# Second cross attention: the row of negated maxima by a matmul with the identity

## What is computed

```python
qn = layernorm(x, ln_q_g, ln_q_b)
q = qn @ Wq * scale                    # 16 heads of 64
k, v = jnp.split(media @ Wkv, 2, axis=-1)
sim = jnp.einsum('bhid,bhjd->bhij', q, k)
sim = jnp.where(media_mask[:, None, None, :], sim, neg_inf)
attn = jax.nn.softmax(sim, axis=-1)
out = jnp.einsum('bhij,bhjd->bhid', attn, v)
```

## Time and profile before

| | |
|---|---|
| median of 3 runs | 3642.56 us |
| profiled execution, span | 3628.6 us |
| TensorE busy in the span | 3390.8 us (93%) |
| VectorE busy | 2019.1 us (56%) |
| ScalarE busy | 1846.1 us (51%) |
| GpSimd busy | 1589.9 us (44%) |
| diagonals of the stage (L1823) | 64, median 1349 ns |

### The profile page before, as it was taken

One profiled execution on the slowest core, in us unless ns is written; L12 is line 12 of the kernel. 1 busy time (PEld: TensorE's weight loads), 2 busy tenths in 40 slices (PEclk: granted clock), 3 DMA queues, 4 the chain that ended last, 5 costly groups with the idle time before them and its releaser, 6 DMA issues. The chain is left out here.

```text
span 3628.6 us, 74082 instructions
## 1 busy us (share of the span) xinstructions
PE 3390.8 (93%) x25048; PEld 2305.3 (64%) x25048; DVE 2019.1 (56%) x3324; ACT 1846.1 (51%) x3374; POOL 1589.9 (44%) x1421
## 2 busy tenths in 40 slices
PE   7798799898999799989999999999999998999997
PEld 5556544344444388866666666666666666878886
DVE  4465577776777454435555555555555553114454
ACT  2254277676776533335555555555555553333333
POOL 3213012221221011107777777777777775005554
PEclk9899799999999899999999999999999999999998
DMA  4784200000000222220000000000001003220200
GB/s 120 170 131 120 79 7 18 17 17 17 17 18 27 96 74 100 107 112 10 13 31 14 32 13 32 16 30 15 33 29 42 13 13 119 82 75 1 98 7 12
DMA packets 74751, 179.36 MB, mean 49 GB/s; under 512 B 14720, under 2 KB 44928, under 8 KB 68480
## 3 DMA queue, kind: packets, MB, share of 16 engines
q1 hardware_dynamic: 70240, 161.81, 14.7%
q0 software_dynamic: 4128, 12.60, 1.3%
HBM read 115.09 MB, written 59.26 MB: 48 GB/s over the span
## 5 line engine op out<-in xcount | busy, mean ns | idle before, releaser
L1654 POOL TENSOR_TENSOR cross_acc<-cross_acc,cross_probs 128x512 f32<-128x512 f32 (+1 forms) x704 | 921.4, 1309 | 159.9 <-ACT cross_probs L1717 118.6
L1717 ACT ACTIVATE cross_probs<-cross_s,cross_bias 128x512 f32<-128x512 f32 (+1 forms) x832 | 530.3, 685 | 488.9 <-PE cross_s L1936 487.1
L1813 DVE TENSOR_REDUCE cross_partmax<-cross_r 128x1 f32<-128x400 f32 (+1 forms) x1024 | 541.2, 570 | 334.3 <-PE cross_r L1906 316.0
L1256 DVE TENSOR_REDUCE cross_partmax<-cross_m 128x2 f32<-128x800 f32 (+1 forms) x512 | 497.0, 991 | 187.1 <-PE cross_m L1359 186.1
L1167 ACT ACTIVATE cross_probs<-cross_s 128x512 f32<-128x512 f32 (+1 forms) x832 | 453.9, 596 | 150.7 <-PE cross_s L1379 150.4
L1949 PE MATMUL cross_av<-cross_probs,cross_v 128*64 128x256 f32 (+1 forms) x3328 | 459.1, 394 | 0.0
L1949 PEld LDWEIGHTS cross_av<-cross_probs,cross_v 128*64 128x64 f32 (+1 forms) x3328 | 199.5, 136 | 173.2 <-ACT cross_probs L1717 77.3
L1106 POOL TENSOR_TENSOR cross_diag<-c_ident,cross_negmax 128x256 fp32r<-128x256 f32 x128 | 76.0, 615 | 497.6 <-DVE cross_negmax L1264 497.6
L1390 PE MATMUL cross_av<-cross_probs,cross_v 128*32 128x256 f32 (+1 forms) x3328 | 269.0, 395 | 10.2 <-ACT cross_probs L1167 9.0
L1802 DVE TENSOR_TENSOR cross_k_lo<-cross_r,cross_k_hi 128x400 fp32r<-128x400 f32 (+1 forms) x256 | 146.4, 572 | 192.4 <-ACT cross_k_hi L1695 192.4
L1930 PE MATMUL cross_s<-cross_q_hi,cross_k_hi 64*128 64x256 f32 (+1 forms) x1664 | 253.0, 299 | 0.0
(11 more groups left out here) (307 smaller groups left out, 6479.6 us busy)
## 6 DMA issues: line engine op xcount, KB each, us to landing
d_masked_ctx<-tail_ctx_split SPq DMA_DIRECT2D x8, 1602.0 KB, 5.3
d_self_qk<-selfproj_qk_split POOLq DMA_DIRECT2D x32, 256.0 KB, 5.5
self_qs<-d_self_qk SPq DMA_DIRECT2D x64, 128.0 KB, 8.0
self_ks<-d_self_qk SPq DMA_DIRECT2D x64, 128.0 KB, 8.5
d_cross<-tail_pr SPq DMA_DIRECT2D x8, 1024.0 KB, 4.6
cross_qp<-d_cross SPq DMA_DIRECT2D x64, 128.0 KB, 2.4
d_cross<-cross_out SPq DMA_DIRECT2D x64, 128.0 KB, 1.8
tail_attn<-d_cross SPq DMA_DIRECT2D x8, 1024.0 KB, 5.5
```

Of the source, the lines that this page charges most:

```text
L1256: nc.vector.tensor_reduce(partmax[:, :, jt // 2, jt % 2, i:i + 1], m_pair(sets[q], w), AX.X, ALU.max).then_inc(maxed, 1)
L1654: nc.gpsimd.tensor_tensor(acc[0:w, g % 2], left, probs[0:w, slot % NPB], ALU.add).then_inc(added, 1)
L1717: nc.scalar.activation(probs[0:w, (g * KT + t) % NPB], src_, ACT.Exp, scale=XHD ** -0.5, bias=bias[0:w, p, t:t + 1]).then_inc(probs_ready, 1)
L1813: nc.vector.tensor_reduce(partmax[:, m, i:i + 1], r_ps[MAX_BANK[q]][:, 0:KCH[i][1]], AX.X, ALU.max).then_inc(maxed, 1)
```

## The change

`negmax` becomes a tile of two times 128 columns, zeroed once at the start of the stage by VectorE. The reduction that negates the maxima writes its four numbers with a stride: for each query tile t, head 0 into column 0 and head 1 into column 64. This tile is then the weights of a matmul whose moving operand is the identity: the result has the negated maxima of head 0 on partition 0 and of head 1 on partition 64, along the row. It takes one matmul for each t, 128 columns, both operands plain f32. The diagonal, its semaphore and VectorE's wait for `negmax` are gone; the shift waits for `negmax`. VectorE waits, before it writes `negmax`, for the shift of the group before.

```diff
--- before.py
+++ after.py
@@ -1542,8 +1542,7 @@
         k_hi, k_lo = ph.sb("k_hi", [P, 2, NKP], F32R), ph.sb("k_lo", [P, 2, NKP], F32R)
         q_hi, q_lo, shf = (ph.sb(n, [P, 2, S], F32R) for n in ("q_hi", "q_lo", "shf"))
         v = ph.sb("v", [P, 2, KT, 512])
-        partmax, negmax = ph.sb("partmax", [P, 4, NC]), ph.sb("negmax", [P, 4])
-        diag = ph.sb("diag", [P, 2, S], F32R)
+        partmax, negmax = ph.sb("partmax", [P, 4, NC]), ph.sb("negmax", [P, 2, P])
         bias = ph.sb("bias", [P, 2, KT])
         NPB = 8
         probs, acc = ph.sb("probs", [P, NPB, 2, S]), ph.sb("acc", [P, 2, 2, S])
@@ -1555,8 +1554,8 @@
         w_hi_ready, w_lo_ready = ph.sem("w_hi_ready"), ph.sem("w_lo_ready")
         kp_ready, kh_ready, k_ready, vp_ready, v_ready, qh_ready, q_ready = (
             ph.sem(n) for n in ("kp_ready", "kh_ready", "k_ready", "vp_ready", "v_ready", "qh_ready", "q_ready"))
-        max_ready, maxed, negmax_ready, diag_ready, shift_ready, shifted = (
-            ph.sem(n) for n in ("max_ready", "maxed", "negmax_ready", "diag_ready", "shift_ready", "shifted"))
+        max_ready, maxed, negmax_ready, zeroed, shift_ready, shifted = (
+            ph.sem(n) for n in ("max_ready", "maxed", "negmax_ready", "zeroed", "shift_ready", "shifted"))
         s_ready, probs_ready, probs_used, added, av_copied, sum_ready, rsum_ready, out_ready = (
             ph.sem(n) for n in ("s_ready", "probs_ready", "probs_used", "added", "av_copied", "sum_ready", "rsum_ready", "out_ready"))
         NM = 4 * NC
@@ -1778,7 +1777,9 @@
 
             @block.vector
             def _(dve):
-                prime(dve, k_ready, qh_ready, maxed, negmax_ready, diag_ready, shifted)
+                prime(dve, k_ready, qh_ready, maxed, negmax_ready, shifted)
+                nc.vector.memset(negmax[:], 0.0).then_inc(zeroed, 1)
+                dve.wait_ge(zeroed, 1)
                 for part in range(2):
                     cols = slice(part * NP * P, (part + 1) * NP * P)
                     dve.wait_ge(w_hi_ready, part + 1)
@@ -1813,16 +1814,13 @@
                     nc.vector.tensor_reduce(partmax[:, m, i:i + 1], r_ps[MAX_BANK[q]][:, 0:KCH[i][1]], AX.X, ALU.max
                                             ).then_inc(maxed, 1)
 
-                def diagonals(u):
+                def negative_maxima(u):
                     b, p, g, n = u
                     dve.wait_ge(maxed, (n + 1) * NM + PRIME)
-                    dve.wait_ge(diag_ready, n + PRIME)
-                    nc.vector.tensor_reduce(negmax[:], partmax[:], AX.X, ALU.max, negate=True).then_inc(negmax_ready, 1)
-                    dve.wait_ge(negmax_ready, n + 1 + PRIME)
                     dve.wait_ge(shift_ready, n + PRIME)
-                    nc.vector.tensor_tensor(diag[:].rearrange("p j (t s) -> p (j t) s", t=2),
-                                            c["ident"][:].unsqueeze(1).to_broadcast([P, 4, P]),
-                                            negmax[:].unsqueeze(2).to_broadcast([P, 4, P]), ALU.mult).then_inc(diag_ready, 1)
+                    nc.vector.tensor_reduce(negmax[:].rearrange("p t (h x) -> p h t x", h=2)[:, :, :, 0],
+                                            partmax[:].rearrange("p (h t) i -> p h t i", h=2), AX.X, ALU.max,
+                                            negate=True).then_inc(negmax_ready, 1)
 
                 def copy_shift(u):
                     b, p, g, n = u
@@ -1836,7 +1834,7 @@
                         k_low(u, i)
                     for q in range(NM):
                         maxima(u, q)
-                    diagonals(u)
+                    negative_maxima(u)
                     copy_shift(u)
                     for i in range(3):
                         k_low(second, i)
@@ -1854,7 +1852,7 @@
                         k_low(after, 0)
                     for q in range(12, 16):
                         maxima(nxt, q)
-                    diagonals(nxt)
+                    negative_maxima(nxt)
                     if after:
                         k_low(after, 1)
                         k_low(after, 2)
@@ -1909,10 +1907,10 @@
                 def shift(u):
 
                     b, p, g, n = u
-                    pe.wait_ge(diag_ready, n + 1 + PRIME)
-                    for h in range(2):
-                        last = nc.tensor.matmul(r_ps[SHIFT_BANK][:, 0:S], c["sel_r"][:, 2 * h], diag[:, h],
-                                                start=(h == 0), stop=(h == 1))
+                    pe.wait_ge(negmax_ready, n + 1 + PRIME)
+                    for t in range(2):
+                        last = nc.tensor.matmul(r_ps[SHIFT_BANK][:, t * P:(t + 1) * P], negmax[:, t], c["ident"][:],
+                                                start=True, stop=True)
                     last.then_inc(shift_ready, 1)
 
                 def scores(u, s):
```

## The result

Over 20 runs of each, the changed kernel has a median of 3652.18 us (3643.04 to 3663.37) against 3638.62 us before (3626.89 to 3648.37): +13.6 us. The ratio is 1.0040, with a 95% interval of 1.0028 to 1.0052: slower, and clear of the 0.2% that the prediction took for what can be told from no change. The profiled execution's span went from 3628.6 to 3642.3 us, +13.7 us; the mean granted clock of TensorE is 0.973 in both, so the clock explains little of the difference. Of the runs of the kernel before that the fifth to seventh experiments are compared with, one took 10,707.56 us at a mean granted clock of 0.478, and is not in their ratios.

A forecast was written before the change was run, and what follows sets the result against it. The prediction took TensorE's own instructions to bound the stage: 64 x 0.21 = 13.4 us for f32 records, less 0.69 us at the first shift, +12.7 us on 3642.56, gives 3655.3 us. Range 3643 to 3664 us.

The forecast's parts named there:

- What bounds the kernel: In the second cross attention TensorE's own instructions set the pace; it is busy 1350.4 of 1360 us.
- The term of the four records: TensorE's shift: four full-f32 records take 0.55 us against 0.34 for two rounded ones, +0.21 us per shift.
- the sum: All terms together: 64 x 0.21 = 13.4 us, less 0.69 us at the first shift, gives +12.7 us.
- The first shift: Ahead of the loop, TensorE's 0.69 us idle wait for the diagonal goes, once.
- The removal from VectorE, at nothing: 64 diagonals, 86 us together, leave VectorE; costed at nothing because idle time behind the diagonal swallows it.
- The weight loads: At TensorE's shift, f32 weights cost no more to load than rounded ones: 192 ns for L1346, 188 ns for the shift.
- Hidden: Rival: TensorE waits for another engine soon behind the shift, so the added 0.21 us costs nothing; 3641.9 us, chance 0.14.
- Faster through the maxima: Rival: earlier VectorE removes a third of weight-load waits for its maxima, 26.6 us; 3628.7 us, chance 0.06.
- Dearer: Rival: loads of f32 weights just written by VectorE aren't hidden, +0.54 us per shift; 3676.5 us, chance 0.04.
- The level: Whole kernel: 12.7 us added to the median of 3642.56 us gives 3655.3 us.

The follow-up runs named there:

- fifth to seventh experiments: Against the kernel before: changed kernel plus four unread VectorE multiplications per group, 1.0534; rounded 128-column kernel with 65 weight columns, 0.9965; changed kernel with 65 weight columns, 1.0027.
- fourth experiment: Changed kernel with each of the two shift matmuls made twice, eight full-f32 records per group; ratio 1.0119 to the kernel before, step 22.67 us.
- second experiment: Changed kernel with rounded negmax and identity, the identity twice side by side so each call streams 256 columns; ratio 1.0002 to the kernel before.
- third experiment: Changed kernel with one unread VectorE multiplication put back per group at the old diagonal's place; ratio 1.0046 to the kernel before, step 22.22 us.
- first experiment: Changed kernel with negmax and identity as rounded f32, two records of 128 columns per shift; ratio 0.9991 to the kernel before, step 22.01 us.
- sixth experiment: Rounded 128-column kernel with only 65 of negmax's columns loaded as weights and a 65-partition copy; ratio 0.9965 to the kernel before, 3624.22 us.

## Why the prediction was right

**What bounds the kernel.** Right: TensorE. Each record added to the shift was paid in full (fourth experiment), and a VectorE with or without the diagonal gave the same time and the same step (second and third).

**The term of the four records.** Forecast +0.21 us a shift from L1346's pace; the profile has +0.21 us, and 22.22 against 22.02 us from shift to shift. Over 64 shifts 13.4 us, less 0.7 us at the first; measured +13.6 us in the medians. That the two are so close is partly chance: the interval of the ratio stands for 10 to 19 us, and in the profiled executions the time from the first to the last shift grew by 15.8 us (1629.41 to 3028.37 before, 1626.13 to 3040.85 after), while the first shift came 3.3 us earlier. What carries the term is the step, which the traces show group by group. One detail was wrong: the prediction has 0.55 us from the shift's first record to the keys. By the starts of the records it is 0.47 us; the fourth record is followed by the keys after 0.03 us, not 0.11, and the missing 0.08 us stands in the first key record, which opens before its weights are there. The second key record starts where the sum had it.

**The first shift.** Right: the idle 0.69 us in front of it are gone; the shift's first record starts 0.32 us after the start of the key record in front of it, which is 0.35 us long (1625.81 to 1626.13).

**The removal from VectorE, at nothing.** Right, and the idle time went where it was said: in front of L1803 (192.4 us before, 266.9 now) and in front of the copy (69.6 before, 83.9 now). That is 88.8 us more waiting for 83.6 us less work.

**The weight loads.** Right that f32 loads cost nothing extra. Wrong was an aside that the sum doesn't use: that calls of 128 columns, were each column paid once, would save some 0.1 us per shift. The first experiment is that case, and it saved next to nothing (0.52 against 0.53 us to the second key record, a step of 22.01 against 22.00 us), since two *rounded* records of 128 columns are held up by the loads of 128 weight columns. With 65 weight columns the step became 0.11 us shorter (sixth experiment, 21.89 us).

**Rivals.** Hidden: no, by the step of 22.22 us and the fourth experiment. Faster through the maxima: no, their waits stayed at 80 us. Dearer: no, 0.112 us a record behind the first.

**The level.** The forecast was 3655.3 us on a median of 3642.56 from three runs; with 20 runs that median is 3638.62, 3.9 us lower. That is why the forecast lies 3.1 us above the 3652.18 us measured though its distance was, if anything, a little short. The distance, not the level, was what the profile could give.

## What to carry to other kernels

Before work is moved from one engine to another, price it on the engine that receives it at the pace of a row of the same type and shape: here 1.35 us on an engine with 3 us of slack were bought with 0.21 us on the one without. A matmul that only moves numbers should get rounded operands where its result is rounded anyway, and no more weight columns than its output needs. Read the cost of a record from the start of the second one behind it, since here the first opened before its weights were loaded.

## What the runs showed of the hardware

With rounded operands and 128 columns the distance from the shift's second record to the key record behind it was 0.11 us with 128 weight columns (188 ns a load; starts at 2318.86 and 2318.97 in the first experiment) and 0.06 us with 65 (135 ns; 2297.10 and 2297.16 in the sixth). With full f32 the pace was 0.11 us at either width.

GpSimd's additions in this stage had a maximum of 1631 ns before and 1299 ns after the change; the line view gives the duration in ns as min/median/max. Before:

```profile
L1654 POOL TENSOR_TENSOR cross_acc<-cross_acc,cross_probs x704: 1257/1281/1631, 1638.5 to 3049.7; 128x512 f32<-128x512 f32 x160, 65x512 f32<-65x512 f32 x16
```

After:

```profile
L1653 POOL TENSOR_TENSOR cross_acc<-cross_acc,cross_probs x704: 1258/1279/1299, 1632.7 to 3061.9; 128x512 f32<-128x512 f32 x160, 65x512 f32<-65x512 f32 x16
```

Each diagonal of the loop lay over two additions. The one that was already running kept its length, and the next one, which began beside the diagonal, was about a quarter longer: around the diagonal from 2119.66 to 2121.01 us they start at 2119.19 and 2120.54 and take 1.27 and 1.61 us. With the unread multiplication put back (third experiment) the maximum is 1625 ns, so it comes from VectorE's work and not from the rest of the change. The diagonal itself was 1349 ns long where GpSimd was at work and 691 ns at the first shift, where it wasn't. In the loop TensorE waited for no diagonal, and without them the time was the same (second experiment).
